# Attention scores on four array tiles: in every second pair of heads the query halves change places

## What is computed

```python
q = l2norm(q) * qs
k = l2norm(k) * ksc
q, k = rotary_xpos(q, k)
...
sim = jnp.einsum('bhwid,bhwjd->bhwij', bq, bk)
...
sim = jnp.where(mask, -jnp.finfo(sim.dtype).max, sim)
attn = jax.nn.softmax(sim, axis=-1)
out = jnp.einsum('bhwij,bhwjd->bhwid', attn, bv)
```

## Time and profile before

| | us |
|---|---|
| median of 3 runs | 2650.95 (2649.64 to 2651.02) |
| the profiled execution | 2650.9 |
| its span, first to last instruction | 2649.1 |
| PE busy | 2582.9 (98%) |
| DVE busy | 1916.7 (72%) |
| ACT busy | 1702.0 (64%) |
| POOL busy | 1422.8 (54%) |

### The profile page before, as it was taken

How to read it: one execution, slowest core, us unless ns; L and a number is a source line. 1 busy time by engine, 2 the same in 40 slices (tenths; PEclk the granted TensorE clock), 3 DMA queues, 4 the chain that set the end, 5 groups by cost and what they waited for, 6 DMA issues and landing times.

```text
span 2649.1 us, 71437 instructions
## 1 busy us (share of the span) xinstructions
PE 2582.9 (98%) x25088; PEld 2221.2 (84%) x25088; DVE 1916.7 (72%) x3779; ACT 1702.0 (64%) x4184; POOL 1422.8 (54%) x1512
## 2 busy tenths in 40 slices
PE   7999999979999999999999999999999999999998
PEld 5888888868888888887888887888888887888887
DVE  7777777668778887786655556788877878666664
ACT  4666666658777777774444446787877777444442
POOL 7888888567777776662100006777777665000000
PEclk9999999989999999999999999999999999999999
DMA  2111111111111111112111111111111111222221
GB/s 47 39 47 37 45 37 37 42 44 39 52 39 50 39 38 42 56 39 79 50 60 56 53 34 49 38 52 39 50 41 36 42 59 34 80 80 73 77 72 48
DMA packets 167250, 130.39 MB, mean 49 GB/s; under 512 B 24870, under 2 KB 165320, under 8 KB 167093
## 3 DMA queue, kind: packets, MB, share of 16 engines
q1 hardware_dynamic: 164789, 119.81, 14.8%
q0 software_dynamic: 2304, 8.47, 1.1%
HBM read 77.47 MB, written 50.33 MB: 48 GB/s over the span
## 4 chain that ended last, share of the span: by engine, by line
PE 89%; DVE 4%; issue 3%; ACT 2%; POOL 1%; DMA 1%; SPq 0%; POOLq 0%; DVEq 0%; ACTq 0%
PE const_banks L1409 6%; PE const_banks L1411 6%; PE const_banks L1410 6%; PE const_banks L1401 6%; PE const_banks L1402 6%; PE const_banks L1403 6%; PE const_banks L1525 5%; PE const_banks L1463 5%; PE const_banks L1499 4%; PE const_banks L1555 3%; PE const_banks L1428 3%; PE const_banks L1429 3%; PE const_banks L1430 3%; PE const_banks L510 3%; PE const_banks L525 3%
## 5 line engine op out<-in xcount | busy, mean ns | idle before, releaser
L1107 ACT ACTIVATE attn_E<-const_banks,attn_nbias,attn_rn 128x128 f32<-128x128 f32 x1024 | 452.9, 462 | 137.8 <-DVE attn_nbias L1314 137.8
L1014 POOL TENSOR_TENSOR attn_qk<-attn_rot_a,attn_rot_b 128x1024 f32<-128x1024 f32 x128 | 303.3, 2370 | 343.3 <-issue 292.5
L1001 POOL TENSOR_TENSOR ffn_rstd<-ffn_var,const_neg_half 128x4 f32<-128x4 f32 x32 | 32.7, 1022 | 645.6 <-DVE ffn_var L1204 645.6
L1409 PE MATMUL const_banks<-weights_w_hi,attn_xT_hi 128*128 128x512 f32 x768 | 315.0, 410 | 3.8 <-ACT attn_sq L1142 3.3
L1411 PE MATMUL const_banks<-weights_w_hi,attn_xT_lo 128*128 128x512 f32 x768 | 303.4, 395 | 0.0
L1410 PE MATMUL const_banks<-weights_w_lo,attn_xT_hi 128*128 128x512 f32 x768 | 303.2, 395 | 0.0
L1225 DVE SCALAR_TENSOR_TENSOR ffn_gated<-const_banks,weights_b_col,ffn_gate 128x512 f32<-128x512 f32 (+1 forms) x192 | 143.7, 748 | 212.1 <-ACT ffn_gate L1085 204.2
L1401 PE MATMUL const_banks<-ffn_xT_hi,ffn_w_hi 128*128 128x512 f32 x704 | 281.7, 400 | 0.7 <-DVE ffn_gated L1225 0.7
L1402 PE MATMUL const_banks<-ffn_xT_lo,ffn_w_hi 128*128 128x512 f32 x704 | 277.9, 395 | 0.0
L1403 PE MATMUL const_banks<-ffn_xT_hi,ffn_w_lo 128*128 128x512 f32 x704 | 277.8, 395 | 0.0
L1085 ACT ACTIVATE ffn_gate<-const_banks,weights_b_col 128x512 f32<-128x512 f32 x160 | 110.0, 688 | 216.2 <-PE const_banks L1403 215.9
(11 more groups left out here) (181 smaller groups left out, 8003.6 us busy)
## 6 DMA issues: line engine op xcount, KB each, us to landing
attn_x_res<-xa SPq DMA_DIRECT2D x128, 128.0 KB, 4.9
xb<-attn_x_new SPq DMA_DIRECT2D x128, 128.0 KB, 1.7
ffn_x_<-xb SPq DMA_DIRECT2D x128, 128.0 KB
h<-ident_h SPq DMA_DIRECT2D x64, 128.0 KB, 1.7
xa<-ident_n SPq DMA_DIRECT2D x64, 128.0 KB, 1.7
attn_x_<-xa SPq DMA_DIRECT2D x128, 64.0 KB
xa<-ffn_x_new SPq DMA_DIRECT2D x16, 512.0 KB, 3.3
ffn_add<-h SPq DMA_DIRECT2D x16, 512.0 KB, 5.0
```

The source lines that it names most:

```text
L1014: pool.tensor_tensor(qk[:, slot].rearrange("p a n -> p (a n)"), rot_a[:].rearrange("p a h d -> p (a h d)"), rot_b[:].rearrange("p a h d -> ...
L1107: last = act.activation(E[:, r, i], ps_s[:, r, i * P:(i + 1) * P], ACT.Exp, bias=nbias[:, r, i:i + 1], scale=rn[:, slot, h:h + 1], accum_o ...
L1409: pe.matmul(out_, xT_hi[:, slot, k], w.w_hi[:, k, cols], start=(k == 0), stop=False)
```

## The change

In pairs of heads with odd `j` the two halves of the queries change places: the late queries come to stand in partitions 0 to 63 of scores, E, `rn`, `nbias` and sums, the early ones in 64 to 127. The 128-column score product then falls on the one column half of the array for even `j` and on the other for odd `j`. The mask is laid accordingly (`quarters`). `weigh` puts the halves back: for odd `j` it multiplies the columns 64 to 127 of ET into the first half of the result and 0 to 63 into the second, two products of 64 columns in place of one of 128. And since `rn` is a column per head with a query per partition, the clamp `ssm` has to hand over the queries' sums of odd pairs with the halves crossed: one DVE instruction becomes four.

```diff
--- before.py
+++ after.py
@@ -1298,7 +1298,13 @@
                     need(dve, s["rn_done"], 2 * b)
                     dve.tensor_reduce(ss[:], sq[:], AX_X, ALU.add).then_inc(s["normed"], 1)
                     need(dve, s["normed"], 2 * b + 1)
-                    dve.tensor_tensor(ssm[:], ss[:], tiny[:], ALU.max).then_inc(s["normed"], 1)
+                    dve.tensor_tensor(ssm[:, HEADS:], ss[:, HEADS:], tiny[:, HEADS:], ALU.max)
+                    pairs, pairs_m, floor = [ap[:, 0:HEADS].rearrange("p (a b r) -> p a b r", b=2, r=2)
+                                             for ap in (ss, ssm, tiny)]
+                    dve.tensor_tensor(pairs_m[:, :, 0], pairs[:, :, 0], floor[:, :, 0], ALU.max)
+                    for to, of in ((slice(0, HD), slice(HD, P)), (slice(HD, P), slice(0, HD))):
+                        last = dve.tensor_tensor(pairs_m[to, :, 1], pairs[of, :, 1], floor[of, :, 1], ALU.max)
+                    last.then_inc(s["normed"], 1)
                 if layer and step == 1:
                     for r in range(1, GROUP):
                         row_done(dve, layer - 1, g, g // 4, g % 4, r)
@@ -1460,8 +1466,13 @@
                 for j in range(HEADS // 2):
                     for r in range(2):
                         h = 2 * j + r
-                        last = pe.matmul(ps_v[r * HD:(r + 1) * HD, j * P:(j + 1) * P],
-                                         v[:, u, h * HD:(h + 1) * HD], ET[:, r, j], start=True, stop=True)
+                        own, head = slice(r * HD, (r + 1) * HD), v[:, u, h * HD:(h + 1) * HD]
+                        if j % 2 == 0:
+                            pe.matmul(ps_v[own, j * P:(j + 1) * P], head, ET[:, r, j], start=True, stop=True)
+                            continue
+                        pe.matmul(ps_v[own, j * P:j * P + HD], head, ET[:, r, j, HD:P], start=True, stop=True)
+                        last = pe.matmul(ps_v[own, j * P + HD:(j + 1) * P], head, ET[:, r, j, 0:HD], start=True,
+                                         stop=True)
                 last.then_inc(s["o_ps"], 1)
 
             def body(t, i, u, on):
@@ -1539,20 +1550,21 @@
                     for r in range(2):
                         own = slice(r * HD, (r + 1) * HD)
                         eye, rule = c["ident_b"][own, own], c["causal"][own]
+                        quarters = ps_s[:, r].rearrange("p (a q n) -> p a q n", q=4, n=HD)
+                        edge = rule[:, :, 0:HD].rearrange("p (a b) n -> p a b n", b=2)
+                        pe.matmul(quarters[0:HD, :, 0:4:3], eye, edge, start=True, stop=False, skip_group_check=True)
+                        pe.matmul(quarters[HD:P, :, 1:3], eye, edge, start=True, stop=False, skip_group_check=True)
                         if step == 2:
-                            pe.matmul(ps_s[0:HD, r], eye, rule.rearrange("p i n -> p (i n)"),
-                                      start=True, stop=False, skip_group_check=True)
-                        else:
-                            pe.matmul(ps_s[0:HD, r].rearrange("p (i n) -> p i n", n=P)[:, :, 0:HD], eye,
-                                      rule[:, :, 0:HD], start=True, stop=False, skip_group_check=True)
-                        pe.matmul(ps_s[HD:P, r].rearrange("p (i n) -> p i n", n=P)[:, :, HD:P], eye, rule[:, :, 0:HD],
-                                  start=True, stop=False, skip_group_check=True)
+                            for rows_, at in ((slice(0, HD), 1), (slice(HD, P), 3)):
+                                pe.matmul(quarters[rows_, :, at], eye, rule[:, 0:2, HD:P], start=False, stop=False,
+                                          skip_group_check=True)
                     for j in range(HEADS // 2):
                         for r in range(2):
                             part = slice(r * HD, (r + 1) * HD)
-                            pe.matmul(ps_s[0:HD, r, j * P:j * P + HD], qT[part, j, 0:HD], kT[part, j, 0:HD],
+                            few, all_ = (slice(0, HD), slice(HD, P)) if j % 2 == 0 else (slice(HD, P), slice(0, HD))
+                            pe.matmul(ps_s[few, r, j * P:j * P + HD], qT[part, j, 0:HD], kT[part, j, 0:HD],
                                       start=False, stop=True, skip_group_check=True)
-                            last = pe.matmul(ps_s[HD:P, r, j * P:(j + 1) * P], qT[part, j, HD:P], kT[part, j],
+                            last = pe.matmul(ps_s[all_, r, j * P:(j + 1) * P], qT[part, j, HD:P], kT[part, j],
                                              start=False, stop=True, skip_group_check=True)
                     last.then_inc(s["s_ps"], 1)
                 if step == ROWS + 1:
```

## The result

The changed kernel takes 2714.15 us (median of 4 runs, 2711.19 to 2716.36) beside 2650.74 (2649.64 to 2651.02) for the kernel before: 1.024 times as long, with a 95% interval of 1.0225 to 1.0255. The forecast was 2719 in a range of 2694 to 2738. The profiled execution took 2711.19 us, with a span of 2709.4 (2649.1 before) and a mean granted clock of 0.994 in both; so 60.3 us of span are to be explained, and the clock has no part in them.

The account below looks back on a forecast made before the run. The prediction took a ring of DVE and ACT, not PE, to bound the kernel; 2650.9 + 65.0 for 112 clamps + 3 for the others gave 2719 us, range 2694 to 2738.

Parts of the forecast that it names:

- The ring: DVE and ACT from rot_b through squares, sums, clamp, maxima, nbias, exponentials back to rot_b, never entering PE: 10.04 us a step.
- Rival 1: PE is the bound after all, the maxima wait for the last score: gain of 20 us, 2630 us; chance 0.03.
- Part 1: Score matmuls on PE: balanced tiles go from 0.88 to 0.68 us, 0.20 us less a step, hidden.
- Part 2: Weighting of v on PE: each tile goes from 0.88 to 0.92 us, plus 0.04 a step, hidden.
- PE's balance: Scores and weighting together on PE: minus 0.16 us a step, bounds minus 0.20 and plus 0.44, moving no end.
- Part 3: One DVE clamp becomes four between sums and maxima: 0.68 us instead of 0.09, plus 0.58 a step from unrounded durations.
- The input's start alone holds: First crossing clamp on DVE, where only the input's start partition changes: held, 0.20 us, bounds 0.08 and 0.20.
- rival 2: No DVE clamp is held, small instructions simply overlap: 28 us more, 2679 us; chance 0.10.
- 3 (2705): On DVE only a new start of the output holds an instruction: 54 us more, 2705 us; chance 0.13.
- 112 steps at the full price and 3 us for the others: Clamps in 112 steps cost 0.58 us each, 65.0 us; 12 others cost 0 to 7 us, taken as 3.
- rival 4: Crossing clamps last longer than 0.17, or idling PE falls to its lower clock: 2730 to 2750 us; chance 0.10.
- PE's wait for qT near 0.9 us: In the profile after, PE's transposes of E wait near 0.9 us for ACT's copy qT, listed now.

Follow-up runs that it names:

- e3: The changed kernel with its matrix products and mask, but the single clamp of the kernel before: 2649.79 us, 1.0002 of the kernel before.
- e4: The kernel before with the four clamps of the change, its matrix products as before: 2717.11 us, 1.0253 of the kernel before.
- e2: The changed kernel, but both crossing clamps read from partition 64 and write from partition 0, one head each: 2688.85 us, 1.0150 of the kernel before.
- e1: The changed kernel, but its four clamps all start at partition 0 and cross nothing: 2675.72 us, 1.0098 of the kernel before.
- e5: The kernel before with rot_b moved ahead of the second product that normalises E: 2705.03 us, 1.0208 of the kernel before.
- e7: The changed kernel with the queries' three clamps moved behind oT_lo: 2696.76 us, 1.0175 of the kernel before.
- e10: e9 with the first half of rot_b moved ahead of the second reciprocal: 2681.45 us, 1.0118 of the kernel before.
- e9: The changed kernel with the queries' three clamps moved between nbias and oT_lo: 2652.92 us, 1.0013 of the kernel before.
- e6: The changed kernel with rot_b moved ahead of the second product that normalises E: 2652.96 us, 1.0012 of the kernel before.
- e8: e7 with rot_b moved ahead of the second product that normalises E: 2715.21 us, 1.0243 of the kernel before.
- e11: The kernel before with the first half of rot_b moved ahead of the second reciprocal: 2629.77 us, 0.9924 of the kernel before.

## Why the prediction was right, step by step

- *The ring and not PE sets the pace.* Right. PE's part alone is worth nothing (e3, 2649.79), the clamps alone cost everything (e4). Rival 1, which the chain's 89% spoke for, is out; after the change the same view says 49%, with the same ring.
- *Part 1, scores 0.20 shorter.* Right at the end that matters: the last one ends 0.206 earlier behind the first. From first to last start it is 0.155, since the last record is now one of 64 columns.
- *Part 2, weighting plus 0.04.* The end came 0.08 later (0.13 between the first and last starts). 64-column records over 128 rows follow each other at 0.06, as taken, and not at 0.11; the bound of plus 0.44 was far off. PE's balance is so minus 0.13 us a step and not minus 0.16.
- *Part 3, four clamps with starts 0.08, 0.20, 0.20, 0.20 apart.* The mechanism was right, with all three held; its size was 12% too large: 0.084, 0.170, 0.172 and 0.188, so plus 0.52 and not plus 0.58. The step that was mis-sized is "0.17 + 0.03": the clamps of 2 to 4 columns last 0.157, not 0.165, and a held one starts 0.014 behind the end of the last and not 0.03, a figure that I had from instructions of 512 columns. Only the maxima, again a large instruction, start 0.03 behind.
- *The input's start alone holds.* Taken against bounds of 0.08 and 0.20, and right (e2): 0.17. Rivals 2 (nothing held, 2679) and 3 (2705) are out. e1 at 2675.72 is what rival 2 described.
- *112 steps at the full price and 3 us for the others.* Right: 58.6 + 1.7.
- *Nothing on top* (rival 4). Right: the crossing clamps over 64 partitions are not longer than the others, and the granted clock is 0.994 as before, though PE idles more.
- *PE's wait for qT near 0.9 us.* Wrong in its place. PE idles about 0.65 us more in a step (0.74 forecast), but only half of it lies there (the transposes' start behind the last output product went from 0.23 to 0.57 in the median). The rest lies at the projection L1415, which waits for oT_lo (0.54 between starts at 904.10 and 904.64 in the rows above, 0.23 undisturbed): oT_lo stands behind nbias on DVE and became late with it. It changed no end.

The sum was therefore 2650.9 + 60.3 = 2711.2 for the profiled execution, against 2719 forecast: 6.4 us from the clamp's size and 1.3 from the 12 other steps. The median, 2714.15, is 3 us above that execution and 5 below the forecast.

## What to carry to other kernels

Before an engine is relieved, look for the ring that never enters it: its share of the chain says little where waits shorter than a record are hidden, and the lists of who waits for whom, with their counts, say it. Small instructions between two neighbours of such a ring cost their start-to-start distance in every step, twice as much when each starts on other partitions than the last; if only a later reader needs them, put them behind the last instruction that the ring waits for (63 us became 3 here). And see what each displaced instruction will meet on the other engines, since 0.08 us of a shift can cost 0.8.

## What the runs showed of the hardware

**DVE and POOL.** I had not expected that a DVE instruction of 4 or 8 columns can last as long as a POOL instruction. Where one with both inputs in SBUF (a clamp, nbias) started while POOL's product of 128x512 with both inputs in SBUF (1.04 us) was running, it ended 0.015 to 0.021 behind POOL's end in the median: nbias in e5 118 times (0.88 in the median instead of 0.17), the clamp in e7 122 times (0.85 instead of 0.16), the last clamp in e10 75 times (0.99). oT_lo, which reads one input from PSUM, starts in the middle of the same POOL instruction in e9 (908.48, rows above) and keeps its 0.69. In e9 the clamp was first, by 0.01 us in the rows above, and kept its length. It works the other way too: POOL's rotation (128x1024, both inputs in SBUF), started 0.015 behind an E product, lasted 2.90 instead of 2.37 in 119 steps of e5 and 117 of e6 and of e8. The Trainium skill says so ("SBUF — State Buffer", section "Who interferes with whom"): a DVE instruction with two SBUF inputs and a GpSimd instruction that reads SBUF contend, and the one that comes second is blocked until the first has ended. The traces agree for the product, by these ends. They don't for POOL's power of 128x8 (L1020, 1.64 us), which reads SBUF too: in the kernel before, 124 times nbias started within it and never lasted more than 0.171; the row of e11 above is one of these. Of the power, only a first short part is seen to block: the one clamp each in e7, e8, e9 and e10 that started 0.01 us after it lasted 0.21 instead of 0.16, and the next, 0.23 us after it, kept its 0.16. What of a longer POOL instruction's recorded time the block covers, no run here shows.

**Held starts.** What the prediction cited of held instructions was confirmed for inputs too. The price, which is what a forecast needs: 0.07 to 0.09 between the starts of two small DVE instructions that are not held, 0.170 of two that are.
